# Last stage of a two-layer transformer: the turn of the routing weights moved to the next block, the load split in two, VectorE's side work moved ahead of the low half

## The chip, the cores and the metric

One core of a Trainium2 chip runs the whole program. The metric is device time in microseconds: the median of 3 runs. One more execution was profiled; all rows are from that one.

## What is computed

Two transformer layers on 8 x 1024 rows of 256 features, each with attention and a feed-forward network (FFN), all in fp32. The change is in the last stage: the output projection of the second attention, the residual, and the second FFN, a mixture of 8 experts (4 chosen per row) plus a shared expert as wide as 4 of them.

```python
x = x + _layernorm(_L1_attn_ref(...))            # ends in: out @ W_out + b_out
h = _layernorm(x)
scores = softmax(h @ router_w)                   # 8 experts
top_k_indices = top_k(scores + router_bias, 4)   # weights: scores / sum of the chosen
act = silu(h @ gate_w[e]) * (h @ up_w[e])        # 128 wide for each of 8 experts
routed = sum over the chosen e of weight[e] * (act[e] @ down_w[e])
shared = (silu(h @ s_gate_w) * (h @ s_up_w)) @ s_down_w      # 512 wide
x = x + _layernorm(routed + shared)
```

Every expert is computed for every row; the weight of one that was not chosen is zero.

## The kernel before

Eight stages follow each other; the last, `phase_project_ffn`, starts near 2500 us. It takes the rows in 16 blocks of 512 (`B` = 8 pairs, j = 0 and 1). The bodies for j are written out, and blocks 2 to 13 run in a loop of six passes. In a block the FFN passes 12 chunks of 128 hidden features: c = 0 to 3 are the shared expert (`NSH` = 4), c = 4 to 11 the experts.

Every matrix product is made of three (`product`): each operand is split in a high part and a low rest, so a chunk is 12 matmuls of 512 columns for gate and up (`gate_up`, tiles `g_ps`, `u_ps`, two buffers each) and 12 of 256 columns for the down product (`down_product`, tile `f_ps`), which is issued two chunks later. The chain of a chunk goes over four steps: ScalarE makes `gate` (Silu of `g_ps`), VectorE `hid` (product with `u_ps`, and for an expert a second one with the weights `wt`), ScalarE copies `hid` into the high half `hh`, VectorE takes the low half `hl` = hid - hh. TensorE can overwrite a `g_ps`, `u_ps` pair when the first VectorE product has read it (`gu_free`).

Between the chunks of block n stand the steps that prepare block n + 1, each at a fixed chunk, written out by hand on each engine:
- c = 0: TensorE turns the attention rows (`turn_attended`, L2595), ScalarE and VectorE split them (`ah`, `al`); c = 1: TensorE projects (`project`); c = 1 to 4: bias, layer norm, residual, second norm on VectorE, GpSimd (`power`) and ScalarE.
- c = 6: TensorE turns the normalised rows (`turn_normal`, L2613), ScalarE `normal_high` writes `xh` (L2499), VectorE `normal_low` writes `xl` (L2336). c = 7: TensorE makes the router's logits (`logit_product`, L2622 and L2624).
- c = 8: `shift` on VectorE, `exponentials` on ScalarE (with two loads of a function table). c = 9: `choose` on VectorE, the 4 of 8 and their weights (`mask`).
- c = 9 and 10: TensorE turns the attended heads of block n + 2 (`turn_heads`, L2585), VectorE divides them by their denominators (`divide`, L2307 to L2309, two each).
- c = 11: TensorE turns the weights (`turn_choice`, L2634), ScalarE copies them (`routed`, tile `rt`, L2509), SP stores them to the chip's memory and loads them back to all partitions (`route`, L2221 and L2223, 2 MB into `wt`, which lies in `raw`).

All of these turned tiles share one PSUM tile, `w_ps`. `turn_choice` therefore waits for the divides of the block (`att_ready`), and `turn_attended` for `rt_relayed`, which SP gives once `rt` is written. On VectorE the steps stand behind the whole of `hidden(j, c)`, that is behind `hl`; on ScalarE they stand behind `hh`.

## Time and profile before

| | us |
|---|---|
| median of 3 runs | 3638.65 (3637.04 to 3640.52) |
| profiled execution | 3627.51 |
| its span in the profile | 3625.8 |
| TensorE busy | 3035.0 (84%) |
| VectorE busy | 2327.8 (64%) |
| ScalarE busy | 1612.0 (44%) |
| GpSimd busy | 724.3 (20%) |

The shares are of the whole span. A wait in the lists is the time in which an engine had nothing to run, put down to the instruction that ended it. The ends of matmuls are modelled: one that is followed closely is shown to end after the next has begun. PEclk is the granted TensorE clock as a share of 2.4 GHz. In a timeline, brackets show how long the engine was idle before and what released it.

### The profile page before, as it was taken

The numbers are of one execution on the slowest core, as the hardware profiler recorded it, in microseconds if no ns is written. First come the engines' busy times: TensorE is split into PE (matmuls) and PEld (weight loads), VectorE is DVE, ScalarE is ACT, GpSimd is POOL, SyncE is SP. The second block draws the span as 40 slices with busy tenths as digits, with TensorE's granted clock in tenths as the row PEclk, the third lists the DMA queues.
The fourth block names the chain that finished last, engine by engine and source line by source line (L and its number), as shares of the span: only waits on it lengthen the run. The fifth ranks groups of instructions, "written<-read, shape, count | busy, mean of one in ns | idle before, by whom it ended". The sixth has DMA issues, their size and how long they took to land. (4 is left out here: it accounts for less than half of the span.)

```text
span 3625.8 us, 61069 instructions
## 1 busy us (share of the span) xinstructions
PE 3035.0 (84%) x20737; PEld 2199.4 (61%) x20737; DVE 2327.8 (64%) x6372; ACT 1612.0 (44%) x2364; POOL 724.3 (20%) x854
## 2 busy tenths in 40 slices
PE   6859999999997666498674777996799999999998
PEld 5644444444443666397443664554688788788887
DVE  5558999999993777681225883444566665565665
ACT  2324777777774333243003653553334344344343
POOL 0021222221211222144772321221000000000000
PEclk9877999999998788699656997998799999999999
DMA  6885655556552565743765976553233232232331
GB/s 179 233 191 80 93 93 89 95 87 98 82 82 76 179 217 183 244 139 120 165 143 180 284 248 218 178 178 127 65 94 82 59 94 81 65 99 70 74 81 44
DMA packets 408067, 470.08 MB, mean 130 GB/s; under 512 B 90448, under 2 KB 295280, under 8 KB 406640
## 3 DMA queue, kind: packets, MB, share of 16 engines
q1 hardware_dynamic: 396032, 443.24, 47.5%
q0 software_dynamic: 10240, 14.16, 2.2%
q10 hardware_dynamic: 1648, 10.81, 0.8%
q8 instruction: 81, 1.33, 0.2%
q14 instruction: 66, 0.54, 0.0%
HBM read 270.90 MB, written 196.67 MB: 129 GB/s over the span
## 5 line engine op out<-in xcount | busy, mean ns | idle before, releaser
L529 ACT ACTIVATE att_pr<-att_e_ps 128x1024 f32<-128x1024 f32 (+2 forms) x640 | 567.2, 938 | 203.8 <-PE att_e_ps L581 203.6
L557 PE MATMUL att_m_ps<-att_ks,att_qs 63*128 63x512 f32 (+3 forms) x1536 | 466.1, 434 | 41.3 <-PEq L39 32.7
L491 DVE CUSTOM_DVE_ANT_0 att_kept<-att_m_ps,att_causal 128x256 f32<-128x256 f32 (+3 forms) x1024 | 448.6, 488 | 49.2 <-DVEq L39 21.9
L557 PEld LDWEIGHTS att_m_ps<-att_ks,att_qs 63*128 63x128 f32 x1536 | 235.0, 189 | 371.0 <-DVE att_mx L494 147.9
L494 DVE TENSOR_REDUCE att_mx<-att_m_ps 128x1 f32<-128x512 f32 x512 | 323.5, 685 | 21.2 <-PE att_m_ps L557 17.1
L2536 ACT ACTIVATE fin_hh<-fin_hid 128x512 fp32r<-128x512 f32 x192 | 121.3, 632 | 479.7 <-DVE fin_hid L2387 372.2
L601 PE MATMUL att_o_ps<-att_pr,att_vs 128*32 128x512 f32 (+3 forms) x3072 | 329.0, 501 | 3.7 <-issue 1.9
L470 POOL TENSOR_SCALAR_AFFINE_SELECT att_pr<-att_pr 128x256 f32<-128x256 f32 (+1 forms) x384 | 181.3, 484 | 698.4 <-PEq L572 694.8
L581 PE MATMUL att_e_ps<-att_qs,att_ks 64*128 64x512 f32 (+3 forms) x1536 | 269.3, 377 | 5.6 <-PEq L39 2.9
L2280 POOL TENSOR_TENSOR fin_rs<-fin_ve,fin_mhalf 128x4 f32<-128x4 f32 x48 | 48.3, 1007 | 1063.0 <-POOLq L39 1063.0
L2383 DVE TENSOR_TENSOR fin_hid<-fin_gate,fin_u_ps 128x512 f32<-128x512 f32 x192 | 131.7, 686 | 179.0 <-PE fin_u_ps L716 100.1
L2394 DVE TENSOR_TENSOR fin_hl<-fin_hid,fin_hh 128x512 fp32r<-128x512 f32 x192 | 133.0, 693 | 141.2 <-ACT fin_hh L2536 141.2
L716 PE MATMUL fin_f_ps<-fin_fhd,fin_hh 128*128 128x256 f32 x768 | 219.3, 286 | 0.3 <-DVE fin_hl L2394 0.3
L716 PE MATMUL fin_f_ps<-fin_fhd,fin_hl 128*128 128x256 f32 x768 | 217.4, 283 | 0.0
L716 PE MATMUL fin_f_ps<-fin_fld,fin_hh 128*128 128x256 f32 x768 | 216.9, 282 | 0.0
L1905 DVE TENSOR_TENSOR lin_am<-lin_a_ps,lin_tri 128x512 f32<-128x512 f32 x128 | 88.6, 692 | 144.3 <-PE lin_a_ps L1988 144.3
L581 PEld LDWEIGHTS att_e_ps<-att_qs,att_ks 64*128 64x128 f32 x1536 | 150.7, 188 | 38.2 <-ACT att_pr L529 14.3
L716 PE MATMUL fin_g_ps<-fin_xh,fin_fhg 128*128 128x512 f32 x384 | 163.2, 425 | 1.1 <-issue 0.8
L716 PE MATMUL fin_u_ps<-fin_xh,fin_fhu 128*128 128x512 f32 x384 | 160.3, 417 | 0.0
L716 PE MATMUL fin_g_ps<-fin_xh,fin_flg 128*128 128x512 f32 x384 | 159.8, 416 | 0.0
L716 PE MATMUL fin_u_ps<-fin_xl,fin_fhu 128*128 128x512 f32 x384 | 158.5, 413 | 0.0
L716 PE MATMUL fin_g_ps<-fin_xl,fin_fhg 128*128 128x512 f32 x384 | 158.1, 412 | 0.0
(324 smaller groups left out, 7298.2 us busy)
## 6 DMA issues: line engine op xcount, KB each, us to landing
fin_raw<-weights SPq DMA_DIRECT2D x16, 2048.0 KB, 15.5
att_qs<-q_high SPq DMA_DIRECT2D x128, 128.0 KB, 5.6
att_ks<-k_high SPq DMA_DIRECT2D x128, 128.0 KB, 7.2
attended<-att_ot SPq DMA_DIRECT2D x64, 256.0 KB, 2.0
prj_o<-attended SPq DMA_DIRECT2D x16, 1024.0 KB
exp_w<-w SPq DMA_DIRECT2D x128, 128.0 KB
lqk_a<-acc SPq DMA_DIRECT2D x32, 512.0 KB
attended<-lin_ot SPq DMA_DIRECT2D x32, 512.0 KB, 3.2
```

Of the source, the lines that this page charges most:

```text
L470: e.affine_select(out=blk, in_=blk, compare_op=ALU.is_ge, fill=0.0, base=0, pattern=lead + [[1, P]], channel_multiplier=-1).then_inc(maske ...
L491: e.tensor_tensor_reduce(kept[:, n % MBUF, 0:w], m_ps[:, n % MBUF, 0:w], causal[:, BLK - w:], 1.0, -3e38, ALU.add, ALU.max, mx[:, h, at, q ...
L494: e.reduce_max(mx[:, h, at, q:q + 1], m_ps[:, n % MBUF, 0:w], AX.X).then_inc(m_free, 1)
L529: e.activation(out, src, ACT.Exp).then_inc(exp_done, 1)
L557: e.matmul(m_ps[:, (2 * i + n) % MBUF, 0:w], qs[rows, j, p, q * P:(q + 1) * P], ks[rows, j, p, h * BLK:h * BLK + w], start=True, stop=True ...
L581: i = e.matmul(e_ps[:, s % 2, n, m * w:(m + 1) * w], ks[rows, j, p, k * P:(k + 1) * P], qs[rows, j, p, (h + 1) * BLK - w:(h + 1) * BLK], s ...
L601: i = e.matmul(o_ps[32 * hd:32 * hd + 32, BLK - w:BLK], vs[:, j, k, hd * VW:hd * VW + 32], pr[:, u % NPR, hd // 2, hd % 2, 0:w], start=k = ...
L716: i = e.matmul(out, a, b, start=first and n == 0, stop=last and n == len(terms) - 1, **kw)
L1905: e.tensor_tensor(am[:, n % 2, 0:F // 2].rearrange("p (r h) q -> p r h q", h=2), a_ps[:, 0:2, 0:2 * P].rearrange("p r (h q) -> p r h q", h=2),
L2383: product_ = e.tensor_tensor(hid[:, c % 2], gate[:, c % 2], u_ps[:, c % 2], ALU.mult)
L2394: e.tensor_tensor(hl[:, c % 3], hid[:, c % 2], hh[:, c % 3].bitcast(fp32), ALU.subtract).then_inc(hl_ready, 1)
L2536: e.activation(hh[:, c % 3], hid[:, c % 2], ACT.Copy).then_inc(hh_ready, 1)
```

## The change

- `turn_choice` is issued in chunk 0 of the block that uses the weights, between its `gate_up` and the down product of the last block's chunk 10, instead of behind chunk 11 of the block before. `routed` stands on ScalarE behind gate 0, `route` on SP at the start of the block.
- The load of `wt` is two transfers of 1 MB with a semaphore each; VectorE waits for the first ahead of chunk 4, for the second ahead of chunk 8.
- `normal_low` (c = 6), `shift` (c = 8) and the `divide`s (c = 9, 10) stand on VectorE between the product(s) and `hl` of their chunk. `normal_high` on ScalarE stands ahead of `hh` 6. `choose` stays behind `hl` 9.
- The first block's `turn_choice`, `routed` and `route` move from the lines ahead of the loop into its chunk 0.

```diff
                 def route(b, j):
...
-                    e.dma_start(wt[:, j], wt_rows[b, j].unsqueeze(0).broadcast_to((P, E, BLK))
-                                ).then_inc(wt_loaded[j], 16)
+                    for h in range(2):
+                        half = slice(h * E // 2, (h + 1) * E // 2)
+                        e.dma_start(wt[:, j, half], wt_rows[b, j][half].unsqueeze(0).broadcast_to((P, E // 2, BLK))
+                                    ).then_inc(wt_loaded[j][h], 16)
...
                 def body(b, j, prev, back, front):
+                    route(b, j)
                     if front:
                         next_o(*later(b, j, 2))
...
                         residual_kept()
-                        route(*later(b, j, 1))
...
-                def hidden(j, c):
-                    if c == NSH:
-                        e.wait_ge(wt_loaded[j], 16)
-                        take(e, (wt_loaded[j], 16))
+                def hidden(j, c, back, front):
+                    if c in (NSH, NSH + E // 2):
+                        half = wt_loaded[j][(c - NSH) // (E // 2)]
+                        e.wait_ge(half, 16)
+                        take(e, (half, 16))
...
+                    if c == 6 and back:
+                        normal_low(1 - j)
+                    if c == 8 and back:
+                        shift()
+                    if c in (9, 10) and front:
+                        for t in range(2):
+                            divide(2 * (c - 9) + t)
                     e.wait_ge(hh_ready, c + 1)
...
                         e.activation(gate[:, c % 2], g_ps[:, c % 2], ACT.Silu).then_inc(gate_ready, 1)
+                        if c == 0:
+                            routed()
+                        if c == 6 and back:
+                            normal_high(1 - j)
                         e.wait_ge(hid_ready, c + 1)
...
-                        if c == 6 and back:
-                            normal_high(1 - j)
                         if c == 8 and back:
                             exponentials()
-                        if c == 11 and back:
-                            routed()
...
                         gate_up(j, c)
...
+                        if c == 0:
+                            turn_choice(back)
                         if c == 6 and back:
                             turn_normal()
...
-                        if c == 11 and back:
-                            turn_choice(front)
```

The lines of the changed kernel lie one or two to nine further down: `turn_choice` is L2635 there, `xl` L2337, `hid` L2385 and L2389, `hl` L2403, `xh` L2501, `rt` L2511, `gate` L2536, `hh` L2542.

TensorE, from the end of a block into the next one inside the loop: the last down matmuls of chunk 9, the turn of the choice, the first gate matmuls of chunk 0. Before:

```order
L716 MATMUL fin_f_ps<-fin_fhd,fin_hh 128x256
L716 MATMUL fin_f_ps<-fin_fld,fin_hh 128x256
L716 MATMUL fin_f_ps<-fin_fhd,fin_hl 128x256
L2634 MATMUL fin_w_ps<-fin_ident,fin_mask 8x128 x4
L716 MATMUL fin_g_ps<-fin_xh,fin_fhg 128x512
L716 MATMUL fin_g_ps<-fin_xl,fin_fhg 128x512
L716 MATMUL fin_g_ps<-fin_xh,fin_flg 128x512
```

The four transposes stood between the blocks. After the change, the same block's chunk 0, the last up matmuls and the first ones of the down product of chunk 10:

```order
L716 MATMUL fin_u_ps<-fin_xh,fin_fhu 128x512
L716 MATMUL fin_u_ps<-fin_xl,fin_fhu 128x512
L716 MATMUL fin_u_ps<-fin_xh,fin_flu 128x512
L2635 MATMUL fin_w_ps<-fin_ident,fin_mask 8x128 x4
L716 MATMUL fin_f_ps<-fin_fhd,fin_hh 128x256
L716 MATMUL fin_f_ps<-fin_fld,fin_hh 128x256
L716 MATMUL fin_f_ps<-fin_fhd,fin_hl 128x256
```

They have moved behind the 12 gate and up matmuls of the next block.

ScalarE, loop body, chunks 6 and 7 before (gate, high half, `xh`):

```order
L2534 ACTIVATE fin_gate<-fin_g_ps 128x512
L2536 ACTIVATE fin_hh<-fin_hid 128x512
L2499 ACTIVATE fin_xh<-fin_w_ps 128x1024
L2534 ACTIVATE fin_gate<-fin_g_ps 128x512
L2536 ACTIVATE fin_hh<-fin_hid 128x512
```

And the same place in the changed kernel, where `xh` stands ahead of the high half, with the beginning of the next block, where the copy of the choice (`rt`) stands between gate 0 and high half 0:

```order
L2536 ACTIVATE fin_gate<-fin_g_ps 128x512
L2501 ACTIVATE fin_xh<-fin_w_ps 128x1024
L2542 ACTIVATE fin_hh<-fin_hid 128x512
...
L2536 ACTIVATE fin_gate<-fin_g_ps 128x512
L2511 ACTIVATE fin_rt<-fin_w_ps 8x512
L2542 ACTIVATE fin_hh<-fin_hid 128x512
L2481 ACTIVATE fin_ah<-fin_w_ps 128x1024
```

VectorE, chunk 10 of a block, before (two products, low half, two divides, the next chunk's product):

```order
L2383 TENSOR_TENSOR fin_hid<-fin_gate,fin_u_ps 128x512
L2387 TENSOR_TENSOR fin_hid<-fin_hid,fin_raw 128x512
L2394 TENSOR_TENSOR fin_hl<-fin_hid,fin_hh 128x512
L2307 TENSOR_SCALAR fin_den<-fin_w_ps 128x16
L2308 RECIPROCAL fin_rden<-fin_den 128x16
L2309 TENSOR_TENSOR fin_row<-fin_w_ps,fin_rden 128x256
```

And in the changed kernel:

```order
L2385 TENSOR_TENSOR fin_hid<-fin_gate,fin_u_ps 128x512
L2389 TENSOR_TENSOR fin_hid<-fin_hid,fin_raw 128x512
L2308 TENSOR_SCALAR fin_den<-fin_w_ps 128x16
L2309 RECIPROCAL fin_rden<-fin_den 128x16
L2310 TENSOR_TENSOR fin_row<-fin_w_ps,fin_rden 128x256
...
L2403 TENSOR_TENSOR fin_hl<-fin_hid,fin_hh 128x512
```

The low half, which waits for ScalarE, stands behind the divides.

## Rows read from the trace of the kernel before

**Rows 1.** Waits of the last stage: engine, line waited for: us in total, times, longest

```profile
PE fin_w_ps L2634 <- DVE fin_row L2309: 42.3, 14, 3.1
PE fin_w_ps L2622 <- DVE fin_xl L2336: 21.7, 15, 1.6
PE fin_w_ps L2634 <- DVE fin_mask L2369: 4.9, 1, 4.9
```

**Rows 2.** Windows, 8 us from the logit product: length, busy per engine (instructions), PEclk, DMA

```profile
2605.40:2613.40 8.00, 8.00 (x42) 7.11 (x43) 3.30 (x5) 1.49 (x3) 0.00 (x0) 0.79 0.01 2
...
3072.62:3080.62 8.00, 8.00 (x49) 7.12 (x50) 4.11 (x7) 2.69 (x4) 0.00 (x0) 1.00 0.00 0
```

**Rows 3.** Windows, 6 us from the transposes of the choice

```profile
2630.55:2636.55 6.00, 6.00 (x38) 5.27 (x39) 3.21 (x5) 2.41 (x5) 0.00 (x0) 1.00 0.16 29
...
3497.80:3503.80 6.00, 5.86 (x23) 4.58 (x24) 2.37 (x4) 1.70 (x3) 0.00 (x0) 0.72 0.14 26
3558.65:3564.65 6.00, 6.00 (x36) 5.18 (x34) 3.51 (x6) 3.33 (x6) 0.00 (x0) 1.00 0.02 3
```

**Rows 4.** Timeline, TensorE, chunks 8 and 9: start, us, engine, line, operation, tiles

```profile
3008.30 0.63 PE L716 MATMUL fin_g_ps<-fin_xl,fin_fhg 128*128 128x512 f32 x1
...
3013.01 0.39 PE L716 MATMUL fin_g_ps<-fin_xh,fin_fhg 128*128 128x512 f32 x1
3013.24 0.39 PE L716 MATMUL fin_g_ps<-fin_xl,fin_fhg 128*128 128x512 f32 x1
```

**Rows 5.** Timeline, chunks 6 and 7 of the next block, three engines, waits in brackets

```profile
3064.53 1.04 PE L2613 MATMUL fin_w_ps<-fin_ident,fin_row 128*128 128x128 f32 x8
...
3067.47 0.58 ACT L2534 ACTIVATE fin_gate<-fin_g_ps 128x512 f32<-128x512 f32 x1
3069.04 0.69 DVE L2387 TENSOR_TENSOR fin_hid<-fin_hid,fin_raw 128x512 f32<-128x512 f32 x1 [0.15 <-DVE fin_hid L2383]
3070.30 1.01 ACT L2499 ACTIVATE fin_xh<-fin_w_ps 128x1024 fp32r<-128x1024 f32 x1
3070.91 0.28 PE L716 MATMUL fin_f_ps<-fin_fhd,fin_hl 128*128 128x256 f32 x1
3071.34 1.22 DVE L2336 TENSOR_TENSOR fin_xl<-fin_w_ps,fin_xh 128x1024 fp32r<-128x1024 f32 x1 [0.22 <-ACT fin_xh L2499]
3072.62 0.28 PE L2622 MATMUL fin_w_ps<-fin_wr,fin_xh 128*128 128x16 f32 x1 [1.43 <-DVE fin_xl L2336]
```

**Rows 6.** Timeline, end of a block: VectorE in chunk 10, TensorE in chunk 11

```profile
3027.28 0.29 PE L716 MATMUL fin_f_ps<-fin_fhd,fin_hl 128*128 128x256 f32 x1
3028.15 0.69 DVE L2394 TENSOR_TENSOR fin_hl<-fin_hid,fin_hh 128x512 fp32r<-128x512 f32 x1 [0.69 <-ACT fin_hh L2536]
...
3030.08 0.42 DVE L2309 TENSOR_TENSOR fin_row<-fin_w_ps,fin_rden 128x256 f32<-128x256 f32 x1
3030.64 0.60 PE L2634 MATMUL fin_w_ps<-fin_ident,fin_mask 128*8 128x128 f32 x4 [3.08 <-DVE fin_row L2309]
```

**Rows 7.** Timeline, and last the load of the weights by its line, us to landing

```profile
3030.42 0.68 DVE L2383 TENSOR_TENSOR fin_hid<-fin_gate,fin_u_ps 128x512 f32<-128x512 f32 x1
...
3032.50 0.57 ACT L2509 ACTIVATE fin_rt<-fin_w_ps 8x512 f32<-8x512 f32 x1
3033.30 0.31 SPq L2221 DMA_DIRECT2D weights<-fin_rt  x1
3034.78 0.41 SPq L2223 DMA_DIRECT2D fin_raw<-weights  x1
...
3059.76 0.69 DVE L2383 TENSOR_TENSOR fin_hid<-fin_gate,fin_u_ps 128x512 f32<-128x512 f32 x1 [0.33 <-DVEq L39]
...
DMA to landing us min/median/max: 14.0/15.5/18.7
```

**Rows 8.** Timeline, VectorE, the first block

```profile
2565.07 3.36 DVE L2375 TENSOR_TENSOR fin_fld<-fin_raw,fin_fhd 128x3072 fp32r<-128x3072 f32 x1
2571.39 0.69 DVE L2383 TENSOR_TENSOR fin_hid<-fin_gate,fin_u_ps 128x512 f32<-128x512 f32 x1 [2.96 <-PE fin_u_ps L716]
```

More of the change, by code:

```diff
@@ L2148, in phase_project_ffn @@
         rt_stored = ph.sem("rt_stored")
-        wt_loaded = [ph.sem(f"wt_loaded{j}") for j in range(2)]
+        wt_loaded = [[ph.sem(f"wt_loaded{j}{h}") for h in range(2)] for j in range(2)]
         g_ready = ph.sem("g_ready")
@@ L2261, in _ @@
                 e.wait_ge(raw_free, 1)
-                route(0, 0)
                 blocks(body)
@@ L2409, in body @@
                     for c in range(NCH):
-                        hidden(j, c)
+                        hidden(j, c, back, front)
                         if c == 0 and back:
@@ L2426, in body @@
                             result()
-                        if c == 6 and back:
-                            normal_low(1 - j)
-                        if c == 8 and back:
-                            shift()
-                        if c in (9, 10) and front:
-                            for t in range(2):
-                                divide(2 * (c - 9) + t)
                         if c == 9 and back:
@@ L2546, in body @@
                             normalise_x()
-                        if c == 6 and back:
-                            normal_high(1 - j)
                         if c == 8 and back:
                             exponentials()
-                        if c == 11 and back:
-                            routed()
                     take(e, (g_ready, NCH), (hid_ready, NCH))
@@ L2564, in _ @@
                 split(2)
-                routed()
                 blocks(body)
@@ L2693, in _ @@
                     turn_heads(t)
-                turn_choice(True)
                 e.wait_ge(low_ready, 2)
```

## Prediction, made before the changed kernel was run

> **What bounds the kernel now.** The page first: TensorE is the busiest engine, but that is a mean over eight stages. The change touches the last one, so I read the rest from 2560 us on. There the list of waits is short on TensorE's side [rows 1]: it waits 42.3 us in 14 places ahead of the transposes of the choice (L2634) for the last `divide` on VectorE, and 21.7 us in 15 places ahead of the logit product (L2622) for `xl`, plus 4.9 us once, in the first block, for the choice itself. ScalarE and VectorE wait for each other much longer, but TensorE is not held by that. So in this stage TensorE is the bound, and what is to be had are its two waits in each of 16 blocks, and what they draw after them.
>
> What they draw is in the windows. In the 8 us from the start of the logit product the granted clock is 0.79 in 11 of the 15 blocks and 1.00 in four [rows 2]; in the 6 us from the choice's transposes on it is 0.72 in 11 of the 14 steady blocks [rows 3]. The last window, 3558.65, where TensorE had no wait ahead of the same four transposes, has 1.00. The timeline shows the price: a gate matmul at the lower level (1.2 GHz) takes 0.63 us, one at 2.4 GHz 0.39, and the next one starts after 0.23 [rows 4]. 8 us at 0.79 are 8 x 0.21 = 1.7 us lost, 6 us at 0.72 are 6 x 0.28 = 1.7 us; where the lower clock fell on part of a wait it cost nothing, so I take 1.6 us for each.
>
> **The change, part by part.** I follow the two blocks between 2963 and 3098 us and call a chunk's gate and up matmuls G(c), its down product D(c). 12 chunks pass in a block, and D(c) is issued behind G(c+2).
>
> *normal_high and normal_low (chunk 6).* Before, ScalarE makes gate 6 at 3067.47 (0.58), waits for VectorE's second product (3069.04 + 0.69), copies hh, and only then `xh` at 3070.30; `xl` starts at 3071.34 and TensorE, done at 3071.03, takes up the logits at 3072.62 [rows 5]. The transposes for `xh` were over by 3065.6 (3064.53 + 1.04), so with `xh` ahead of the wait it runs 3068.05 to 3069.1, while VectorE is still multiplying; `xl` can start at 3069.8 and end at 3071.0. That is the time at which TensorE comes free. The wait (21.7 us in 15) goes, and with it 0.16 us each that the modelled end of a matmul hides (the last one starts at 3070.91 and takes 0.28, but the next could start 0.12 later, half of the 0.23 for half the columns): 24.1 us. As `xl` arrives with nothing to spare I leave 0.1 us each: **22.6 us** gained. hl 6 now stands behind `xl` and ends near 3071.7, which costs nothing: D(6) is issued behind the logits and G(8), from 3075.6 on.
>
> *divide and choose (chunks 9, 10), and the turn of the choice.* Before, the four `divide` and the choice run behind hl; the last one starts at 3030.08 and TensorE goes on at 3030.64 [rows 6]. VectorE waits 0.7 us for hh in each chunk, the row at 3028.15 among them. In the new place two divides (0.8 us each) fill that gap in chunks 9 and 10, and hl 10 (0.6 us) comes behind them: the last divide ends near 3028.4 instead of 3030.5. That alone leaves a third of the wait. The other part is the move of `turn_choice` behind G(0) of the next block: TensorE goes from D(9), whose last matmul starts at 3027.28, at 3027.4 straight into G(0) (12 x 0.23 = 2.8 us) and needs the divides and the choice at 3030.2, 1.8 us after they are there. G(0) itself needs the first product of chunk 10, which ends a multiply and the two divides ahead of that, before 3026. So the wait goes whole: 42.3 us and 14 x 0.16 = **44.5 us**. What is late next: hl 9 and hl 10 come 1 us and more later than now, but D(10) is only issued at 3030.6, and hl 10 is there at 3029.1.
>
> *The clock.* With both waits gone nothing of what preceded the 22 slow stretches is left but the 1.8 us of 16-column logit matmuls. 22 x 1.6 = **35 us**.
>
> *routed, route, turn_attended (chunk 0).* This is where the change adds a wait on the path. The copy of the turned choice is now due between gate 0 and hh 0 on ScalarE, and `turn_attended` needs it read (`rt_relayed`, by way of SP). VectorE starts product 11 at 3029.1, 1.3 us earlier than now; rt starts 2.08 us after it now (3030.42 and 3032.50, with hh 11 between) [rows 7], and has gate 0 (0.58) ahead of it as well then: 3029.1 + 2.08 + 0.58 + 0.57 = 3032.3 is its end. Now SP's store is issued 0.23 us after that end (3032.50 + 0.57 and 3033.30), so TensorE is released near 3032.6. It is through with D(10) at 3027.4 + 2.8 + 0.4 (the four transposes) + 1.4 (12 x 0.12) = 3032.0 to 3032.1. A new wait of 0.5 us in 14 blocks: **7 us** lost. Queued behind it are `turn_attended`, G(1) and the projection; ScalarE's `ah` follows, and VectorE's `al` needs it 2 us before the projection does. On ScalarE hh 0 stands behind rt, but product 0 is not done earlier. On SP the relay stands ahead of `next_o`, which has the time until chunk 9.
>
> *Weights in two parts.* Before, the load is issued at 3034.78 and first read at 3059.76, 25 us later; it lands after 14.0 to 18.7 us [rows 7]. In the new order store and load follow rt: store issued 3032.55, load 3034.05 (1.48 later, as now), while chunk 4 comes at 3027.4 + 27.0 + 0.5 = 3054.9, the 27.0 being 3059.76 less the start of G(0) (3030.64 + 0.45) and 1.6 of slow clock. 20.9 us for the first four experts, against at most 18.7 for all eight: nothing on the path. The second issue costs SP 0.4 us, which nobody waits for.
>
> The Trainium skill, DMA: Bandwidth & Descriptors, section Two DMAs through the same engine are not ordered, says that descriptors start in order but that nothing orders transfers across the engines. So the split may not bring the first half in much ahead of the second. By an even share the first half would be there after some 8 us, by the rule perhaps only after the whole 18.7; the sum is the same, but the rival on late weights keeps its chance.
>
> *First block.* TensorE waits 4.92 us for the choice while G(0) could run. VectorE's split of the down weights (2565.07, 3.36 us) then bounds: product 0 can start at 2568.5 instead of 2571.39 [rows 8]. **3 us** gained, between 0 (if the copy of the choice, later by a table load, holds `turn_attended`) and 5.
>
> *Sum.* 22.6 + 44.5 + 35 + 3 - 7 = 98 us. The profiled execution took 3627.51 us (span 3625.8), so it would take 3529; the median of the runs is 3638.65, 0.3% higher, and 98 off it gives **3540.6 us**. Per block: from a mean of 66.7 us (3497.80 less 2630.55, over 13 [rows 3]) to about 66.7 - 1.5 - 3.2 - 2.5 + 0.5 = 60.0 (the clock's 35 us over 14 blocks).
>
> **The rivals.**
> First, *the clock still falls behind the logits.* The traces never show the narrow matmuls without the wait ahead of them, so what they do alone is open. For it: in 11 of 15 blocks the fall came just there. Against it: in four blocks, the one at 3072.62 with 1.43 us of wait among them, the same matmuls left the clock at 1.00. If all 11 stay, 11 x 1.6 = 18 us are not gained: 3558.
> The Trainium skill, TensorE: Matmul & The Clock Gate, Part 1, says that recent activity releases the clock and that idleness lowers it, and Part 4 that transposes do not count as busy as other matmuls do. By Part 1 removing the waits is right and gives the 3540; the rows after the two waits agree so far (0.79 and 0.72 behind them, 1.00 where there was none).
>
> Second, *the relay binds.* If rt comes a whole step later (ScalarE takes it behind work that VectorE is late with, 3 us as now between the hidden product's end and the next gate), 14 x 3 = 42 us are lost and the time is about 3583; above 2 us the clock may fall there too. Against it: the chain above is made of rows and misses by tenths.
>
> Third, on the other side, *the weights are late.* The first product of chunk 4 waits for the first half. It decides from 20.9 us from issue to landing, and the whole gain is eaten when each of 16 blocks waits 6.1 us, from 27 us on; at 30 us the time is 3540 + 16 x 9.1 = 3686. The longest landing in the trace is 18.7 us with the `o` load (1 MB) behind it, as it would be.
>
> Fourth, *it does not do it*: VectorE, with hl put back in chunks 6, 8, 9 and 10, becomes what TensorE waits for, and waits of the same size reappear before D or G. VectorE would have to lose its 1.8 us of margin in every block, and it does no more work than before. Then about 3635.
>
> **How the numbers follow.** Forecast 70%, own range 3525 (no relay wait, 5 us in the first block, a few us of scatter) to 3552. Clock 15% at 3558, relay 7% at 3583, not doing it 4%, late weights 4%. The range 3525 to 3572 holds the first two with the relay at up to twice its price on top, and leaves out some 15%. Faster by over 0.2% (7 us, about what a measurement of this kernel can tell from no change): 92%; within it 4%; slower 4%.
>
> **What would show it.** Right: no wait ahead of L2635 (the choice's new line), under 0.2 us ahead of the logits, about 0.5 us ahead of `turn_attended`, granted clock 1.00 through the blocks, block period 60.0. The clock rival shows as 0.79 in the windows behind the logits with no wait. Late weights show as a wait ahead of the second product of chunk 4, a binding relay as a wait over 1 us at `turn_attended`. I am wrong above all if the periods stay over 62 us with the named waits gone: then the bound was not where I read it.

## The result, and the profile after

| | before | changed |
|---|---|---|
| median, us | 3637.85 (4 runs, 3636.17 to 3640.52) | 3527.56 (4 runs, 3521.61 to 3529.06) |
| profiled execution, us | 3627.51 | 3526.91 |
| its span, us | 3625.8 | 3525.2 |
| last stage of that execution, us | 1078.85 | 974.41 |

The ratio is 0.9693, with a 95% interval of 0.9676 to 0.9710. The changed kernel is 110 us faster by the medians. 3527.56 us is 13 us below the forecast of 3540.6 and just inside the range, which began at 3525.

The last line of the table is the yardstick of all that follows. It is the span less the start of the first transposes of normalised rows (L2613 before, L2614 in the changed kernel). The stages ahead of that point are the same code in all kernels here, and yet it comes anywhere between 2543 and 2563 us in the twelve profiles, so a span alone says little about a few microseconds. The length of the last stage repeats to 0.5 and 0.7 us in the two kernels that were profiled twice.

First the list of waits of TensorE in the last stage of the changed kernel, from 2565 us on, with one row of VectorE's. The columns are those of [rows 1].

```profile
DVE fin_hid L2385 <- issue: 13.4, 5, 2.8
...
PE fin_w_ps L2596 <- PEq L39: 2.9, 1, 2.9
...
PE fin_w_ps L2635 <- DVE fin_mask L2370: 2.3, 1, 2.3
...
PE fin_w_ps L716 <- DVE fin_al L2317: 2.0, 5, 0.5
```

The 42.3 us in 14 and the 21.7 us in 15 of [rows 1] have no successor: TensorE waits nowhere at the choice's transposes in the 14 steady blocks, nor at the logits. What is left are two single waits in the first block, and one kind that nobody forecast, ahead of the projection; it is shown below with VectorE's row.

The windows that answer to [rows 2] and [rows 3]: 8 us from the logit product, 6 us from the transposes of the choice in two blocks, 8 us in the first block, and all the rest of the stage. The last three columns are the granted clock, the share of the DMA engines and GB/s.

```profile
3023.25:3031.25 8.00, 8.00 (x51) 7.11 (x50) 4.99 (x11) 2.70 (x4) 0.00 (x0) 1.00 0.00 0
2987.30:2993.30 6.00, 6.00 (x42) 5.40 (x41) 3.41 (x5) 3.72 (x6) 0.00 (x0) 1.00 0.17 55
3046.59:3052.59 6.00, 6.00 (x42) 5.41 (x41) 2.02 (x3) 2.89 (x5) 0.00 (x0) 1.00 0.18 52
2570.00:2578.00 8.00, 5.50 (x19) 4.72 (x20) 4.86 (x4) 2.49 (x4) 0.00 (x0) 0.57 0.36 66
2580.00:3525.20 945.20, 930.70 (x5688) 825.34 (x5687) 619.51 (x1617) 409.03 (x670) 46.37 (x46) 1.00 0.34 85
```

0.79 and 0.72 have become 1.00, and the last row says it for the whole: from 2580 us to TensorE's last matmul, at 3512.6, the clock is at 2.4 GHz. Where TensorE did 42 instructions in 8 us behind the logits, it does 51. The choice's transposes start at 2630.59 in the second block and at 3403.82 in the fifteenth, 13 periods of 59.48 us; before it was 66.7.

Chunk 6 of the changed kernel, the place of [rows 5]. The timeline, three engines.

```profile
3019.80 0.58 ACT L2536 ACTIVATE fin_gate<-fin_g_ps 128x512 f32<-128x512 f32 x1
...
3020.28 1.02 ACT L2501 ACTIVATE fin_xh<-fin_w_ps 128x1024 fp32r<-128x1024 f32 x1
...
3021.37 0.69 DVE L2389 TENSOR_TENSOR fin_hid<-fin_hid,fin_raw 128x512 f32<-128x512 f32 x1 [0.15 <-DVE fin_hid L2385]
3021.98 1.22 DVE L2337 TENSOR_TENSOR fin_xl<-fin_w_ps,fin_xh 128x1024 fp32r<-128x1024 f32 x1
...
3023.11 0.28 PE L716 MATMUL fin_f_ps<-fin_fhd,fin_hl 128*128 128x256 f32 x1
3023.25 0.28 PE L2623 MATMUL fin_w_ps<-fin_wr,fin_xh 128*128 128x16 f32 x1
```

`xh` runs while VectorE multiplies, `xl` follows the product at once and ends at 3023.2, when TensorE comes to the logits: 0.14 us after the start of its last down matmul, against 1.71 in [rows 5].

The end of a block, the place of [rows 6] and [rows 7]: the last divide, the first gate matmul of the next block, product 11, high half 11, gate 0, the choice's transposes, its copy, SP's store and the attention transposes that wait for the copy.

```profile
2984.51 0.40 PE L716 MATMUL fin_g_ps<-fin_xh,fin_fhg 128*128 128x512 f32 x1
2984.68 0.42 DVE L2310 TENSOR_TENSOR fin_row<-fin_w_ps,fin_rden 128x256 f32<-128x256 f32 x1
...
2985.63 0.68 DVE L2385 TENSOR_TENSOR fin_hid<-fin_gate,fin_u_ps 128x512 f32<-128x512 f32 x1
...
2987.18 0.63 ACT L2542 ACTIVATE fin_hh<-fin_hid 128x512 fp32r<-128x512 f32 x1 [2.58 <-DVE fin_hid L2389]
2987.30 0.60 PE L2635 MATMUL fin_w_ps<-fin_ident,fin_mask 128*8 128x128 f32 x4
...
2987.72 0.58 ACT L2536 ACTIVATE fin_gate<-fin_g_ps 128x512 f32<-128x512 f32 x1
...
2988.20 0.57 ACT L2511 ACTIVATE fin_rt<-fin_w_ps 8x512 f32<-8x512 f32 x1
...
2989.00 0.30 SPq L2221 DMA_DIRECT2D weights<-fin_rt  x1
...
2989.17 1.04 PE L2596 MATMUL fin_w_ps<-fin_ident,fin_row 128*128 128x128 f32 x8
```

The divides end 2.2 us ahead of the transposes that wait for them. The copy ends at 2988.77, SP passes it on by 2989.00, and `turn_attended` starts at 2989.17 with no idle time in brackets: the relay is on time by 0.2 us or less.

The weights: the load's line, us from issue to landing, for the 32 halves.

```profile
DMA to landing us min/median/max: 8.7/12.7/17.0
```

No product of chunk 4 or 8 waits for them: in the block shown the load is issued at 2990.48, 1.5 us behind the store, and product 4 starts at 3012.09, 21.6 us later.

What was not foreseen stands at the blocks with which a pass of the loop begins. VectorE and, in the last row, TensorE.

```profile
3050.45 0.69 DVE L2385 TENSOR_TENSOR fin_hid<-fin_gate,fin_u_ps 128x512 f32<-128x512 f32 x1 [2.62 <-issue]
...
3052.75 1.23 DVE L2317 TENSOR_TENSOR fin_al<-fin_w_ps,fin_ah 128x1024 fp32r<-128x1024 f32 x1
...
3054.03 0.38 PE L716 MATMUL fin_w_ps<-fin_wh,fin_ah 128*128 128x256 f32 x1 [0.34 <-DVE fin_al L2317]
```

For 2.6 us VectorE has its data (gate 0 was made at 3047.01) and starts nothing. "issue" is time in which the profile shows nothing to wait for. It happens five times, once for each jump back between the six passes, and each time `al` is 0.3 to 0.5 us late for the projection.

The first block, the place of [rows 8].

```profile
2568.89 3.36 DVE L2376 TENSOR_TENSOR fin_fld<-fin_raw,fin_fhd 128x3072 fp32r<-128x3072 f32 x1
...
2569.02 0.60 PE L2635 MATMUL fin_w_ps<-fin_ident,fin_mask 128*8 128x128 f32 x4 [2.30 <-DVE fin_mask L2370]
2572.50 1.94 PE L2596 MATMUL fin_w_ps<-fin_ident,fin_row 128*128 128x128 f32 x8 [2.88 <-PEq L39]
```

TensorE does G(0) while VectorE chooses, waits 2.30 us for the choice, and then 2.88 us for the relay. `rt` was there at 2570.2, but SP only stored it at 2572.42: `route(0, 0)` now stands behind a wait of SP's for the end of VectorE's split of the down weights (`raw_free`), which ends at 2572.25. The clock goes with the waits: it stands at 1.2 GHz again until 2577 (0.57 over the 8 us above), so that from the start of `turn_attended` to that of the projection TensorE needs 5.89 us, where before it needed 3.85.

### The profile page after: what moved, and what is told of

It reads as the page before. It is cut to its first block and busy times, and to the rows that moved or that the text cites. A ratio compares the mean times of both kernels' runs of the same rounds, so it can differ in the third digit from the quotient of the medians.

```text
span 3525.2 us, 61125 instructions
## 1 busy us (share of the span) xinstructions
PE 2996.3 (85%) x20737; PEld 2172.5 (62%) x20737; DVE 2320.0 (66%) x6372; ACT 1611.4 (46%) x2364; POOL 727.7 (21%) x854
## 5 line engine op out<-in xcount | busy, mean ns | idle before, releaser
L494 DVE TENSOR_REDUCE att_mx<-att_m_ps 128x1 f32<-128x512 f32 x512 | 323.3, 684 | 21.6 <-PE att_m_ps L557 17.5
L2542 ACT ACTIVATE fin_hh<-fin_hid 128x512 fp32r<-128x512 f32 x192 | 121.4, 632 | 417.0 <-DVE fin_hid L2389 319.3
L2385 DVE TENSOR_TENSOR fin_hid<-fin_gate,fin_u_ps 128x512 f32<-128x512 f32 x192 | 131.6, 685 | 134.0 <-ACT fin_gate L2536 71.3
L2403 DVE TENSOR_TENSOR fin_hl<-fin_hid,fin_hh 128x512 fp32r<-128x512 f32 x192 | 132.5, 690 | 105.9 <-ACT fin_hh L2542 100.8
L716 PE MATMUL fin_g_ps<-fin_xh,fin_fhg 128*128 128x512 f32 x384 | 156.1, 407 | 0.0
L716 PE MATMUL fin_u_ps<-fin_xh,fin_fhu 128*128 128x512 f32 x384 | 152.3, 397 | 0.0
L716 PE MATMUL fin_g_ps<-fin_xh,fin_flg 128*128 128x512 f32 x384 | 152.0, 396 | 0.0
L716 PE MATMUL fin_u_ps<-fin_xl,fin_fhu 128*128 128x512 f32 x384 | 151.1, 394 | 0.0
## 6 DMA issues: line engine op xcount, KB each, us to landing
fin_raw<-weights SPq DMA_DIRECT2D x32, 1024.0 KB, 12.7
```

Of the source, the lines that this page charges most:

```text
L494: e.reduce_max(mx[:, h, at, q:q + 1], m_ps[:, n % MBUF, 0:w], AX.X).then_inc(m_free, 1)
L716: i = e.matmul(out, a, b, start=first and n == 0, stop=last and n == len(terms) - 1, **kw)
L2385: product_ = e.tensor_tensor(hid[:, c % 2], gate[:, c % 2], u_ps[:, c % 2], ALU.mult)
L2403: e.tensor_tensor(hl[:, c % 3], hid[:, c % 2], hh[:, c % 3].bitcast(fp32), ALU.subtract).then_inc(hl_ready, 1)
L2542: e.activation(hh[:, c % 3], hid[:, c % 2], ACT.Copy).then_inc(hh_ready, 1)
```

## Experiments

The stage lengths are in one table; the sections say what each is for. "Less" is against 1078.85 for the kernels made from before, and against 974.41 for those made from the changed one.

| run | median us (runs) | ratio to before, 95% | last stage us | less |
|---|---|---|---|---|
| before, again | 3644.33 (1) | | 1079.34 | -0.5 |
| normal_high and normal_low alone | 3596.86 (3589.51 to 3602.46) | 0.9892 [0.9866, 0.9917] | 1036.55 | 42.3 |
| turn of the choice and split load alone | 3602.28 (3586.17 to 3604.36) | 0.9890 [0.9855, 0.9925] | 1041.21 | 37.6 |
| placement alone | 3539.08 (3531.86 to 3547.78) | 0.9736 [0.9706, 0.9765] | 986.84 | 92.0 |
| changed, one load | 3537.08 (1) | | 975.5 | -1.1 |
| changed, relay first in block 0 | 3529.64 (1) | | 972.44 | 2.0 |
| changed, loop written out | 3525.74 (3524.67 to 3527.36) | 0.9696 [0.9678, 0.9713] | 970.89 | 3.5 |
| changed, relay late | 3577.16 (1) | | 1018.54 | -44.1 |
| changed, again | 3525.24 (5) | 0.9706 [0.9684, 0.9728] | 975.15 | -0.7 |
| loop written out, relay first, split early | 3520.55 (5) | 0.9697 [0.9681, 0.9713] | 967.3 | 7.1 |

### What scatters, and what doesn't: before, run again

> The kernel before, unchanged, once more with a profile. Its first profiled execution took 3627.5 us, 10 us less than the median of its runs (3637.9), while that of the changed kernel took what its runs take. Theory: the missing 10 us are falls of the clock: in that profile 22 of the 29 waits ahead of the logits and the choice drew one, at 1.7 us each, and usually it is more of them. Then this profile shows a time between 3627 and 3640 and 22 to 29 stretches at 1.2 GHz behind the two waits, 1.7 us longer for each one more. Rival: the difference lies in an earlier stage; then the last stage takes 1079 us again, whatever the whole takes.

The span was 3642.6 us, 16.8 longer than the profiled execution of before. The last stage began at 2563.26 instead of 2546.95 and took 1079.34 instead of 1078.85, although there were 23 slow stretches behind the two waits where there had been 22. The one more was made up by the first block, in which the clock rose earlier: from the start of the stage to the turn of the normalised rows in block 0 it took 49.18 us, not 50.63. So 16.3 of the 16.8 us lie in the seven stages that the change doesn't touch; the expectation's theory fell and its rival held. From here on the stage's length is compared, and a single run suffices where the stage moves by well over 1 us.

### normal_high and normal_low alone

The two moves of chunk 6, in the kernel before.

```diff
+                    if c == 6 and back:
+                        normal_low(1 - j)
                     e.wait_ge(hh_ready, c + 1)
...
                         e.activation(gate[:, c % 2], g_ps[:, c % 2], ACT.Silu).then_inc(gate_ready, 1)
+                        if c == 6 and back:
+                            normal_high(1 - j)
                         e.wait_ge(hid_ready, c + 1)
```

> The kernel before with one part of the change: normal_high ahead of the high half and normal_low ahead of the low half of chunk 6. Theory (TensorE is the bound, each wait costs itself and the fall of the clock behind it): the wait ahead of the logits (21.7 us in 15, 24.1 from start to start) and the 11 or more falls behind it (19 us) go, the waits ahead of the choice stay at 3.0 us: 43 us less than before, up to 48 if the clock usually falls more often. Rival (the wait moves: VectorE is only made late elsewhere): within 10 us of before, with a wait of the same size ahead of the choice or a down product.

Its list of waits, and two windows: 8 us from the logit product and 6 us from the choice's transposes.

```profile
PE fin_w_ps L2634 <- DVE fin_row L2309: 43.1, 14, 3.2
```

```profile
3310.45:3318.45 8.00, 8.00 (x51) 7.12 (x50) 4.70 (x9) 2.80 (x4) 0.00 (x0) 1.00 0.00 0
```

```profile
3334.11:3340.11 6.00, 5.75 (x22) 4.46 (x23) 2.26 (x4) 1.71 (x3) 0.00 (x0) 0.72 0.03 8
```

The wait ahead of the logits is gone, and with it every fall of the clock behind them: 1.00 in all 15 windows. The choice's wait stays, 43.1 us in 14, and so do the falls behind it, in 10 of 14. This answers the first rival: the narrow matmuls alone lower the clock in none of 15 blocks. The stage is 42.3 us shorter, as expected (43). Of this 24.1 are the wait and 0.4 the first block; 0.8 more wait ahead of the choice and 0.5 more of stops at the jumps of the loop go off. The 19.1 us left are 12 falls of the clock fewer (10 for 22), 1.6 us each.

### The turn of the choice alone

Only the move of `turn_choice`, `routed` and `route` and the load in two parts; `divide` and `normal_low` stay behind `hl`.

```diff
                         gate_up(j, c)
+                        if c == 0:
+                            turn_choice(back)
...
-                        if c == 11 and back:
-                            turn_choice(front)
```

> The changed kernel with everything on VectorE and ScalarE in chunks 6 to 10 put back behind the low and high halves: only the turn of the choice in chunk 0 and the load in two parts are left. Theory: the wait ahead of the choice goes (44.5 us and 19 us of clock), that ahead of the logits stays. Without the placement VectorE comes to product 11 some 2 us later, so the relay of the copied choice should hold turn_attended for 1 to 1.5 us in 14 blocks: 63 less 14 to 21, so 42 to 49 us less than before. Rival (placement matters for the logits alone): no wait at turn_attended and 63 us less.

TensorE's waits, and the slowest of the windows behind the logits.

```profile
PE fin_w_ps L2623 <- DVE fin_xl L2337: 20.2, 15, 1.6
PE fin_w_ps L2596 <- PEq L39: 17.7, 15, 2.9
PE fin_w_ps L2635 <- DVE fin_row L2310: 3.2, 11, 0.6
PE fin_w_ps L716 <- DVE fin_al L2317: 3.0, 5, 0.8
```

```profile
2935.57:2943.57 8.00, 8.00 (x30) 6.89 (x31) 1.92 (x3) 1.23 (x2) 0.00 (x0) 0.57 0.00 0
```

The wait at the choice shrinks from 42.3 us to 3.2, but a part of it comes back one step later: `turn_attended` now waits 1.06 us in each of 14 blocks (17.7 less the first block's 2.9), because VectorE, with the divides behind `hl`, comes to product 11 that much later, and gate 0, `rt` and SP follow it. This is the relay term of the prediction, and here it is real. The clock no longer falls behind the choice (1.00 in all windows there), and falls behind the logits in 10 of 15 blocks, in two of them for longer (0.57 and 0.59 over 8 us, where the others have 0.79). The sum: 44.5 of the choice, less 14.8, 3.2 and 3.0 of the other waits and 4.8 that modelled ends hide (0.16 in each of the 30), plus 1.5 of shorter waits ahead of the logits and 0.2 in the first block, plus 11 x 1.7 = 18.7 behind the choice, less 1.7 for the falls behind the logits (ten, two of them double, against eleven) = 37.4. Measured: 37.6. The expectation, 42 to 49, was missed: it had the relay right, but left out the waits of 3.2 and 3.0 us and the double falls.

### The placement alone

The changed kernel with `turn_choice` put back behind chunk 11, `routed` and `route` with it, and one load. What is left are the steps between product and `hl`.

```diff
-                        if c == 0:
-                            turn_choice(back)
...
+                        if c == 11 and back:
+                            turn_choice(front)
```

> The kernel before with the placement alone (normal_high, normal_low, shift and the divides ahead of the high or low half), the turn of the choice still behind chunk 11, one load. Theory: the logits' wait goes with its falls (43 us), the wait ahead of the choice shrinks from 3.1 to about 1 us (29 us less); whether the clock still falls behind 1 us of wait and four transposes is open: 72 us less than before if it does, about 91 if it does not. Rival (the turn's place carries the gain there): the wait ahead of the choice stays over 2.5 us and the time 43 us under before.

The wait at the choice, and a window behind it.

```profile
PE fin_w_ps L2634 <- DVE fin_row L2309: 8.8, 14, 0.8
```

```profile
2922.55:2928.55 6.00, 5.71 (x37) 4.85 (x37) 2.46 (x5) 1.59 (x3) 0.00 (x0) 1.00 0.02 4
```

The placement alone brings 92.0 of the 104.4 us; the expectation had about 91 for the case that the clock doesn't fall. The divides, 2 us and more earlier, leave 0.6 us of wait in each block instead of 3.0, where the prediction had left a third of it (1 us), and 0.6 us ahead of four transposes don't lower the clock: 1.00 in all 14 blocks. So the whole gain of the clock comes with the placement, and the turn of the choice, the larger part of the diff, brings the last 12.4 us: 8.8 of wait, 2.2 that modelled ends hide (14 x 0.16), 0.2 in the first block and 1.3 of stops of TensorE at the jumps back, less 2.8 of the new waits ahead of the projection, which make 9.7. 2.7 us of the 12.4 I can't place. The 12.4 us are shown by the stage's length; the ratios of the times, 0.9736 and 0.9693, have intervals that still touch.

### One load instead of two

```diff
-                    for h in range(2):
-                        half = slice(h * E // 2, (h + 1) * E // 2)
-                        e.dma_start(wt[:, j, half], wt_rows[b, j][half].unsqueeze(0).broadcast_to((P, E // 2, BLK))
-                                    ).then_inc(wt_loaded[j][h], 16)
+                    e.dma_start(wt[:, j], wt_rows[b, j].unsqueeze(0).broadcast_to((P, E, BLK))
+                                ).then_inc(wt_loaded[j], 16)
```

> The changed kernel with the weights loaded in one transfer of 2 MB again, waited for ahead of chunk 4. The last stage, from the first transposes of the normalised rows (L2614) to the end of the span, repeats within 0.5 us in two profiles of the kernel before (1078.9 and 1079.3), so it is compared rather than the whole. Theory (20 us between issue and use, 19 at most to land): the last stage stays within 1 us of 974.4, with no wait ahead of the second product of chunk 4. Rival (the split is what makes the late turn affordable): a wait ahead of that product in some blocks, 1 to 5 us each, and a longer stage.

From issue to landing, by the load's line:

```profile
DMA to landing us min/median/max: 13.9/15.6/17.2
```

No wait at chunk 4, and a stage 1.1 us longer, where "within 1" was expected. 0.6 of it are longer waits for `al` behind the jumps back (2.6 us instead of 2.0), and the two profiles of the changed kernel differ by 0.7, so it isn't clear of scatter. The split is not needed here: 17.2 us is less than the 21.6 that there are. It does bring its shorter landings (8.7 at the least), which nothing uses.

### The relay first, in the first block

```diff
                     e.wait_ge(rt_stored, 16)
+                    if isinstance(b, int) and b == 0 and j == 0:
+                        e.wait_ge(raw_free, 1)
...
                 residual_kept()
-                e.wait_ge(raw_free, 1)
                 blocks(body)
```

> The changed kernel with SP's one-time wait for raw_free (the whole of the down weights split) put behind the relay and the store of the first block, ahead of its load. In the changed kernel TensorE waits 2.9 us at the first turn_attended although rt is there at 2570.2: SP issues the store only at 2572.4, when the split is over. Theory (SP's queue holds the relay): the store follows rt by 0.2 us, the 2.9 us shrink to under 1, and the last stage gains what VectorE's ah and al leave of it, 1 to 2 us. Rival (ScalarE or VectorE hold the block): the wait goes but the stage stays at 974.4 within 0.5.

The wait ahead of `turn_attended` fell from 2.9 us to 0.8, and the stage by 2.0 us. This shows where most of the first block's gain had gone: into SP's order.

### The loop written out

```diff
-                with e.Fori(1, B - 1) as b:
+                for b in range(1, B - 1):
```

The same on all five engines.

> The changed kernel with the loop over the middle 12 blocks of the last stage written out instead of six passes of two. In the changed kernel VectorE stands for 2.6 us at each pass back (13.4 us in 5, released by nothing in the profile), and TensorE then waits 0.3 to 0.5 us for al. Theory (the pass back costs VectorE its instructions): the 2.6 us and the 5 waits for al go, the last stage gains 2 to 3 us. Rival (the stop is not the branch): both stay where they are. Code that is written out may stop elsewhere; then the gain is smaller.

TensorE's whole list of waits from 2565 us on:

```profile
PE fin_w_ps L2596 <- PEq L39: 2.9, 1, 2.9
PE fin_w_ps L2635 <- DVE fin_mask L2370: 2.3, 1, 2.3
PE fin_f_ps L716 <- DVE fin_hl L2403: 0.3, 1, 0.3
```

and VectorE at the block that began at 3047 in the changed kernel too, product 0 with nothing ahead of it:

```profile
3047.36 0.68 DVE L2385 TENSOR_TENSOR fin_hid<-fin_gate,fin_u_ps 128x512 f32<-128x512 f32 x1
```

Without the jumps back the stops of VectorE are gone, and so are the five waits ahead of the projection. The stage is 3.5 us shorter, a little more than expected (2 to 3). 2.9 of it lie in the five blocks behind a jump, 2.8 of them the waits; the rest, 0.1 us in each of the five blocks that end in a jump, is there in both profiles of the changed kernel, so it isn't scatter, and what costs it stays open. That the stop belongs to the jump is shown; what the engine does in it is not.

### The relay late

`routed` behind high half 0 instead of ahead of it: a step later on ScalarE, which is the second rival's case.

```diff
-                        if c == 0:
-                            routed()
...
                         e.activation(hh[:, c % 3], hid[:, c % 2], ACT.Copy).then_inc(hh_ready, 1)
+                        if c == 0:
+                            routed()
```

> The changed kernel with ScalarE's copy of the turned choice behind high half 0 instead of ahead of it: about 1.5 us later. It prices the relay, which in the changed kernel costs nothing although the prediction gave it 7 us. Theory (it is just in time, the store issued at 2989.0 and turn_attended begun at 2989.17): nearly all of the delay appears as a wait of TensorE at turn_attended, 1.2 to 1.6 us in 14 blocks, last stage 991 to 998. Rival (there is room, a us or more): last stage within 5 us of 974.4.

Its waits, a block with a jump back (TensorE, then ScalarE), a window there, and a window behind one of the other blocks.

```profile
PE fin_w_ps L2596 <- PEq L39: 35.7, 15, 4.9
```

```profile
2827.37 1.51 PE L2596 MATMUL fin_w_ps<-fin_ident,fin_row 128*128 128x128 f32 x6 [4.17 <-PEq L39]
```

```profile
2826.09 0.63 ACT L2540 ACTIVATE fin_hh<-fin_hid 128x512 fp32r<-128x512 f32 x1 [3.84 <-DVE fin_hid L2385]
2826.62 0.57 ACT L2511 ACTIVATE fin_rt<-fin_w_ps 8x512 f32<-8x512 f32 x1
```

```profile
2827.37:2833.37 6.00, 6.00 (x21) 5.11 (x22) 1.41 (x2) 1.62 (x2) 0.00 (x0) 0.61 0.53 93
2890.08:2896.08 6.00, 6.00 (x40) 5.48 (x41) 2.64 (x4) 2.88 (x4) 0.00 (x0) 1.00 0.45 101
```

Both expectations missed: 44.1 us were lost, more than either. They had taken all blocks alike, and they are not. In nine blocks the relay comes 1.1 to 1.5 us late and nothing else happens. In the five that follow a jump back, `rt` stands behind a high half that stands behind VectorE's stop, TensorE waits 3.9 to 4.2 us, and the clock falls (0.58 to 0.61 over 6 us, 2.3 to 2.5 us lost). The sum: 30.8 of waits in 14 blocks, 2.0 more in the first, 2.2 hidden by modelled ends, 12.2 of clock in the five, less the 2.8 at the projection, which are gone: 44.4.

### The changed kernel again, and the three repairs together

The changed kernel on another chip, and beside it a kernel with the loop written out, the relay first in block 0, and VectorE's and ScalarE's split of the down weights moved ahead of `shift` and `exponentials` of the first block.

```diff
                 normal_low(0)
+                split(2)
                 shift()
                 for t in range(TPB):
                     divide(t)
                 choose()
-                split(2)
...
                 normal_high(0)
-                exponentials()
                 split(2)
+                exponentials()
```

> The changed kernel, unchanged, beside the next one and on the same chip, with a second profile. If the last stage is as repeatable in it as in the kernel before, it takes 974.4 us within 0.5 again, while the whole scatters by several us with the earlier stages; the time is 0.969 of the kernel before.

> The changed kernel with three small edits that the runs point to: the middle blocks written out, SP's wait for raw_free behind the first relay, and in the lines ahead of the first block the split of the down weights (ScalarE's copy ahead of the exponentials, VectorE's difference ahead of shift), where both engines wait for TensorE. Theory: 3.5 us for the first as measured, 2.0 for the second as measured, 1 to 2 for the third (the 3.4 us of the difference leave the way to product 0, but shift comes 1.2 us later): last stage 967 to 969, 6 us less than the changed kernel, 0.17% of the whole, hardly above the scatter of the medians. Rival (the second and third lie under the same wait, the first block being held by al): 969 to 971.

The first block of the combined kernel on TensorE, and then the 6 us from the start of `turn_attended`, first with the relay alone, then combined:

```profile
2575.33 0.60 PE L2636 MATMUL fin_w_ps<-fin_ident,fin_mask 128*8 128x128 f32 x4 [1.25 <-DVE fin_mask L2371]
2576.73 1.07 PE L2597 MATMUL fin_w_ps<-fin_ident,fin_row 128*128 128x128 f32 x8 [0.80 <-PEq L39]
```

```profile
2575.09:2581.09 6.00, 5.73 (x22) 4.58 (x23) 4.77 (x5) 2.03 (x3) 0.00 (x0) 0.72 0.38 92
2576.73:2582.73 6.00, 6.00 (x40) 5.46 (x41) 3.13 (x4) 2.60 (x4) 0.00 (x0) 1.00 0.46 102
```

The changed kernel repeats: 975.15 us of stage (expected within 0.5 of 974.4, and 0.2 more than that), and a ratio of 0.9706 beside the first 0.9693. The combined one has a stage of 967.3 us: 3.5 for the loop, 2.0 for the relay, and what is left for the earlier split is 1.6. TensorE waits 1.25 us for the choice instead of 2.30, and the relay's wait is the 0.80 of the relay alone; in exchange it stands 2.2 us ahead of `turn_heads`, where it stood 1.2 before the split was moved, and `turn_attended` starts 0.7 us later in the stage than with the relay alone. What the split wins comes from the clock: behind the shorter wait it stays at 1.00, where with the relay alone it fell to 0.72 over 6 us, and from `turn_attended` to the projection it takes 3.70 us instead of 5.73 (0.3 of that a wait). In time it is 3520.55 (3515.77 to 3525.71) against 3525.24 (3514.30 to 3534.23), and 0.9697 against 0.9706: the intervals overlap, and the gain, 7 to 8 us by the stage's length and 5 by the medians, is shown by the first alone.

## Why the prediction was right, and where it was off

The forecast was faster, by 98 us, with no wait of a steady block left but a small one. The mechanism held in all its main steps: both waits gone, the clock at 2.4 GHz without a break behind the first block, the period from 66.7 to 59.48 us (60.0 forecast), the weights on time. The stage became 104.4 us shorter. Term by term:

| term | forecast | measured | from |
|---|---|---|---|
| wait ahead of the logits | 22.6 | 24.1 | no wait; the 0.1 us left over in each block was not used |
| wait ahead of the choice | 44.5 | 44.5 | no wait in 14 blocks |
| clock | 35 | about 38 | the rest of the sum; 22 x 1.7 = 37.4 |
| first block | 3 | 0.5 | start of the stage to the turn of the normalised rows, 50.63 and 50.08 |
| relay ahead of `turn_attended` | -7 | 0 | no wait in 14 blocks |
| `al` late behind a jump back | not seen | -2.8 | 2.0 of wait, 0.16 hidden in each of 5 |
| sum | 98 | 104.4 | |

**The relay** is the step that failed, by 7 us. The chain behind it was right in each link: from product 11 to `rt` 2.57 us (2.66 was forecast), from the copy's end to SP's store 0.23 us. What was wrong was its start. I had put the last divide 1.0 us behind the start of G(0) and product 11 1.7 us behind it; the rows show 0.59 for the divide's end and 1.12 for the product. From the first product of chunk 9 to the end of the last divide VectorE took 10.51 us, as forecast (10.59), but it began that stretch 9.92 us ahead of G(0) and not 9.59. Most of this is `shift`, which the change also moved and for which the prediction had no term. ScalarE's exponentials used to stand idle for it; two rows, before and changed:

```profile
3015.64 0.23 ACT L2504 ACTIVATE fin_sc<-fin_ls 128x32 f32<-128x32 f32 x1 [0.29 <-DVEq L2345]
```

```profile
2972.42 0.23 ACT L2506 ACTIVATE fin_sc<-fin_ls 128x32 f32<-128x32 f32 x1
```

From high half 8 to gate 9 it is 3.76 us in all 15 blocks before and 3.49 in the changed kernel; no run moves `shift` alone. Half a microsecond is all that the term was, and that margin was there. The two neighbours of this kernel show that the term was no phantom: with the divides behind `hl` it is 1.06 us a block, with `rt` a step later 1.1 to 1.5 where no jump precedes, and 3.9 to 4.2 behind a jump.

**The clock** was taken at 1.6 us a stretch, below the 1.7 that both windows gave, for falls that might overlap a wait. They don't: 22 x 1.7 = 37.4 fits the rest, which also holds 0.8 us of TensorE's stops at three jumps of the loop before. As a remainder of the sum this is worked out, not measured by itself; the kernel with `normal_high` and `normal_low` alone comes to 1.6 each.

**The first block** gave 0.5 us of the 3, less than the 1.45 by which it differs between the two profiles of before, so no gain is shown there. VectorE's part came as forecast: product 0 was 2.7 us earlier in the stage (24.44 and 21.78). The prediction named the copy of the choice as the danger and saw it in a table load; it was there at 2570.2, as hoped. It was held on SP, where `route(0, 0)` came to stand behind the one-time wait for `raw_free`. I had worked out what each queue the step was moved past would lose, but not what a wait already on the queue would cost the step. And I had no term for the clock: `turn_attended` was still 2.5 us earlier, and TensorE lost 2.0 of it behind the two waits, at 1.2 GHz.

**The jump back** was in no sum. Before, VectorE waits for TensorE at the start of each steady block, 2.7 to 2.9 us at four of the five jumps, so that a stop of 2.6 us is not in the list there. Filling the gaps made VectorE early, and the stop came out as a wait. The trace of before shows a stop of this kind once in the whole stage (2.81 us ahead of the product at 3369.72, behind a jump back too), and I had passed over it; at the other jumps the same idle time is put down to TensorE, for which VectorE had to wait as long. With the placement alone all five show (13.3 us in all).

**The rivals.** The clock rival fell in the kernel that takes the wait alone away: 15 windows of 1.00. The relay one would have been real at a step later, and dearer than its 42 us (44.1, through the blocks behind a jump). Late weights have 4.6 us to spare (21.6 less 17.0), and one load would have done. The fourth, a VectorE that TensorE waits for elsewhere, came only as the `al` of 0.3 to 0.5 us behind a jump.

**The median.** Of the 13 us between 3540.6 and 3527.56, 6.4 are the terms above. 0.8 are the median of before, which was 3638.65 of three runs and is 3637.85 of four. The rest lies ahead of the stage, as far as the profiles show it: the sum was made against the profiled execution, whose early stages were short (the repeat's took 16 us longer), and carried to the median of before. Their scatter is in no term of mine, and why these stages scatter stays open.

## What to carry to other kernels

When a wait ends on an engine that itself stands idle for another one in each step, look first for work that can be put into that idle time; here a handful of steps put there brought 92 of 104 us, and moving the waiting instruction the rest. Price what a wait draws behind it (here a slower clock, worth 37 us beside 69 of waits), and read from a block without the wait that it goes when the wait goes. Before a step is moved, list the waits already queued ahead of its new place, one-time ones too, and check the blocks at the jump of a loop apart from the others: slack that you use up had been hiding something there.

## What the runs showed of the chip

- **A jump back stops VectorE for 2.6 to 3.0 us.** Five times in the changed kernel (2.62 us at 3050.45), 2.97 us at the most with one load, and with the loop written out none over 0.4 us. Before it was covered at four jumps of five by a wait of 2.7 to 2.9 us.
- **Waits of one length lower the clock in one place and not in another.** A wait of 1.2 to 1.6 us ahead of the 16- and 8-column logit matmuls lowered it in 11 of 15 blocks, one of 1.1 to 1.5 us ahead of `turn_attended` in none of nine (relay late) and one of 1.06 in none of 14 (turn of the choice alone), 0.6 to 0.8 us ahead of the choice's transposes in none of 14; 2.8 to 3.1 us there lowered it in 11 of 14, and in 13 of 14 when before ran again; 3.9 us and more ahead of `turn_attended` in five of five. The logit matmuls with no wait ahead lowered it in none of 15.
- **Half a broadcast load is not half the time.** Of two parts of 1 MB, issued 0.6 us apart, each lands after 8.7 to 17.0 us (median 12.7); 2 MB in one lands after 13.9 to 17.2 (15.6).
